# A four-block graph transformer on one core: edge counts built in SBUF, the output product woven into the next head, ten places for the turned count rows

## What is computed

```python
def _sparse_attention(x, src, dst, wq, bq, wk, bk, wv, bv, wo, bo):
    N, D = x.shape
    H, Dh = (NUM_HEADS, D // NUM_HEADS)
    q = (x @ wq + bq).reshape(N, H, Dh) * Dh ** (-0.5)
    k = (x @ wk + bk).reshape(N, H, Dh)
    v = (x @ wv + bv).reshape(N, H, Dh)
    scores = jnp.einsum('ehd,ehd->eh', q[src], k[dst])
    smax = jax.ops.segment_max(scores, src, num_segments=N)
    ex = jnp.exp(scores - smax[src])
    denom = jax.ops.segment_sum(ex, src, num_segments=N)
    attn = ex / denom[src]
    out = jax.ops.segment_sum(attn[:, :, None] * v[dst], src, num_segments=N)
    return out.reshape(N, D) @ wo + bo
...
for i in range(NUM_BLOCKS):
    y = _cond_layer_norm(x, cond, s1_w[i], s1_b[i], b1_w[i], b1_b[i])
    y = _sparse_attention(y, src, dst, wq[i], bq[i], wk[i], bk[i], wv[i], bv[i], wo[i], bo[i])
    x = x + y
    y = _cond_layer_norm(x, cond, s2_w[i], s2_b[i], b2_w[i], b2_b[i])
    y = jax.nn.relu(y @ m_w1[i] + m_b1[i]) @ m_w2[i] + m_b2[i]
    x = x + y
```

## Time and profile before

| what | us |
|---|---|
| median of 3 runs | 3600.6 |
| lowest and highest | 3591.68, 3606.22 |
| the profiled execution | 3616.84 |
| its span in the trace | 3615.1 |
| sorting, to the first one-hot tile | 144.8 |
| group loop | 247.2 |
| exchange, to the first product of block 0 | 112.2 |
| a block (the second of four) | 512.0 |
| graph layers | 1072 |

### The profile page before, as it was taken

The page is one execution under the profiler, slowest core; times in us unless marked ns, Lnnn a source line. Parts: engine busy times, 40 slices in busy tenths (PEclk is TensorE's granted clock), DMA queues, the critical chain, the costliest instruction groups (busy, mean ns, idle before and its releaser), DMA issues.

```text
span 3615.1 us, 31865 instructions
## 1 busy us (share of the span) xinstructions
PE 3073.9 (85%) x12190; PEld 1990.3 (55%) x12190; DVE 1745.2 (48%) x3292; ACT 749.7 (21%) x1046; POOL 832.6 (23%) x622
## 2 busy tenths in 40 slices
PE   4877349999899998999998899998286598898999
PEld 0344236777457766556676567765144355565555
DVE  9968324554235455234553245552288788412111
ACT  0132121222212222112222212222110211212221
POOL 5623121334223333213343213342010100000100
PEclk9988669999999999999999999999589599799899
DMA  4011210000000000100000100000435445201000
GB/s 139 5 32 30 76 54 12 1 24 1 30 26 12 1 24 18 36 14 1 24 1 18 38 12 1 24 1 29 104 111 151 128 131 148 61 14 56 12 0 29
DMA packets 83679, 147.31 MB, mean 41 GB/s; under 512 B 22047, under 2 KB 22438, under 8 KB 83528
## 3 DMA queue, kind: packets, MB, share of 16 engines
q1 hardware_dynamic: 61604, 121.16, 10.9%
q0 software_dynamic: 20624, 20.99, 2.1%
q10 hardware_dynamic: 1300, 3.13, 0.3%
HBM read 126.95 MB, written 30.37 MB: 44 GB/s over the span
## 4 chain that ended last, share of the span: by engine, by line
PE 67%; DVE 12%; issue 7%; DMA 4%; DVEq 4%; ACT 4%; POOL 1%; SPq 1%; POOLq 0%; ACTq 0%
PE ps L1269 14%; PE ps L1278 11%; PE ps L1362 9%; PE ps L1464 7%; PE ps L1419 4%; DVEq L912 3%; DMA typed_t<-run,rowi 3%; PE ps L1350 3%; DVE big L910 3%; PE ps L1351 3%; PE ps L1353 3%; PE ps L1352 3%; PE ps L1335 2%; PE ps L1456 2%; PE ps L1303 2%
## 5 line engine op out<-in xcount | busy, mean ns | idle before, releaser
L576 POOL TENSOR_TENSOR pacc<-pacc,prob 125x628 f32<-125x628 f32 (+1 forms) x288 | 405.4, 1408 | 301.2 <-DVE prob L862 301.2
L1278 PE MATMUL ps<-yT,w 128*128 128x416 f32 (+1 forms) x1152 | 407.0, 513 | 5.4 <-ACT yT L1077 5.4
L1362 PE MATMUL ps<-prob,big 125*128 125x314 f32 x1280 | 394.3, 429 | 11.1 <-DVE prob L862 11.1
L1464 PE MATMUL ps<-pieces,counts_r 125*125 125x512 f32 x1400 | 361.1, 414 | 27.3 <-DVE x L937 15.6
L834 DVE CUSTOM_DVE_ANT_0 ps<-ps,mneg 125x628 f32<-125x628 f32 x320 | 260.1, 823 | 243.9 <-PE ps L1335 243.9
L1115 ACT ACTIVATE prob<-ps 125x628 f32<-125x628 f32 x320 | 222.2, 694 | 710.9 <-PE ps L1353 710.9
L1464 PEld LDWEIGHTS ps<-pieces,counts_r 125*125 125x125 f32 x1400 | 264.0, 190 | 120.2 <-DVE x L937 22.3
L862 DVE SCALAR_TENSOR_TENSOR prob<-prob,ct 125x628 f32<-125x628 f32 x320 | 274.2, 857 | 95.6 <-ACT prob L1115 95.6
L1278 PEld LDWEIGHTS ps<-yT,w 128*128 128x128 f32 x1152 | 216.8, 189 | 187.0 <-issue 178.9
L1269 PE MATMUL ps<-w,yT 128*125 128x512 f32 x640 | 291.3, 602 | 11.5 <-DVE pieces L924 10.8
L1269 PE MATMUL ps<-w,big 128*125 128x512 f32 x640 | 282.9, 601 | 3.7 <-issue 3.0
(11 more groups left out here) (196 smaller groups left out, 4215.1 us busy)
## 6 DMA issues: line engine op xcount, KB each, us to landing
basis<-in_basis SPq DMA_DIRECT2D x240, 256.0 KB, 2.6
w<-in_m_w SPq DMA_DIRECT2D x8, 1024.0 KB, 6.7
typed_t<-zero_row SPq DMA_DIRECT2D x20, 305.2 KB
ct<-typed_t POOLq DMA_DIRECT2D x2, 3051.8 KB, 42.8
w<-in_wv SPq DMA_DIRECT2D x5, 1024.0 KB, 5.4
w<-in_wq SPq DMA_DIRECT2D x5, 1024.0 KB, 5.2
w<-in_wk SPq DMA_DIRECT2D x5, 1024.0 KB, 5.7
oT<-in_cw SPq DMA_DIRECT2D x9, 512.0 KB, 6.2
```

The costliest lines, as they stand in the source:

```text
L576: nc.gpsimd.tensor_tensor(pacc[:, c0:c0 + nn], pacc[:, c0:c0 + nn], prob[:, n % 3, p0:p0 + nn], ALU.add).then_inc(psum_done, 1)
L1278: last = mm(lin_ps(job, 128, nn), weight[:, k, m * 128:(m + 1) * 128], lhs[:, k, c0:c0 + nn], start=(k == 0), stop=(k == KD - 1))
L1362: last = mm(o_halves[:, b, :], vrow[:, t, h * DH:(h + 1) * DH], prob[:, n % 3, b * QUARTER:(b + 1) * QUARTER], start=(t == 0), stop=(t == ...
L1464: last = mm(lin_ps(job, P, D), counts_r[:, slot, k, :], pieces[:, piece, k, :], start=(self_ is None and k == 0 and piece == 0), stop=(k = ...
```

## The change

Three changes in one. **One:** the counts are built in SBUF. A tensor `typed` of 125 partitions and 2 x 6256 int32 words holds all 20 buckets; its halves are seen as `ct` and as `typed1` in float16, and the second half later as the mask `mneg`. POOL clears it once at the start (a MEMSET of 125x12512). POOL no longer scatters: for each group it loads the place of the group's bucket into a register and copies `run` there (625 int32 words, the place given by the register); a later group of the same bucket overwrites the partial sum. `run` has four places instead of two. The zero rows, the 20 zeroing DMAs, the 59 indirect DMAs and the ten loads are gone; type 1 is written to DRAM (`ct2_d`) by five DMAs, which must have landed before `mneg` overwrites it. In the group loop the four `onehot_dst` of a group are made by one TENSOR_TENSOR of 128x500, and `carry` is made by ACT behind its copy. After the mean layer POOL makes the counts of type 0 by ten subtractions `ct - ct2` in place of the load. **Two:** the ten output products of head h go into the first ten steps of head h + 1, one behind each step, and DVE's additions likewise; the last head's stay where they were. The six projections of head h + 2 are cut in parts of 1, 3 and 2. **Three:** the turned rows have ten places (two in `yT`, eight in `big`, both unused then), and SP, not ACT, starts their DMAs, in its queue behind the five of type 1.

```diff
+PARTS = {None: range(6), 0: range(0, 1), 1: range(1, 4), 2: range(4, 6)}
...
     for h in range(HEADS):
-        project(h + 2)
+        if h:
+            g["out"][h - 1] = [w.take() for _ in range(T)]
+        project(h + 2, 0)
+        project(h + 2, 1)
         max_row(h + 1)
         g["den"][h] = w.take()
-        g["out"][h] = [w.take() for _ in range(T)]
+        project(h + 2, 2)
+    g["out"][HEADS - 1] = [w.take() for _ in range(T)]
...
-            for s in range(2):
-                sp.wait_ge(rows_out[s], 16 * ((GROUPS + 1 - s) // 2))
+            sp.wait_ge(bucket_placed, GROUPS)
             for t in range(0, T, 2):
-                for r, to in ((0, ct), (1, typed1)):
-                    sp.dma_start(to[:, t:t + 2, :], typed_t[r * N + t * P:r * N + (t + 2) * P, :]
-                                 .rearrange("(t p) n -> p t n", p=P)).then_inc(typed_in[t // 2], 16)
+                sp.dma_start(ct2_d[t * P:(t + 2) * P, :].rearrange("(t p) n -> p t n", p=P),
+                             typed1[:, t:t + 2, :]).then_inc(ct2_out[t // 2], 16)
+            for s in range(T):
+                sp.wait_ge(crow_copied, s + 1)
+                sp.dma_start(crow_d[s * P:(s + 1) * P, :], turned_counts(s)).then_inc(crow_out[0 if s < 2 else 1], 16)
...
             drained_inc(consts_set)
+            nc.gpsimd.memset(typed[:], 0)
             pool.wait_ge(payload_ready, 1)
...
-                nc.gpsimd.indirect_dma_start(
-                    out=typed_t, out_offset=bass.IndirectOffsetOnAxis(ap=rowi[0:P, g:g + 1], axis=0),
-                    in_=run[:, g % 2, :], in_offset=None,
-                    bounds_check=2 * N - 1, oob_is_err=False).then_inc(rows_out[g % 2], 16)
+                place = pool.value_load(placei[0:1, g:g + 1], min_val=0, max_val=(PLACE + (T - 1) * N) // 2)
+                if g:
+                    pool.wait_ge(bucket_placed, g)
+                nc.gpsimd.tensor_copy(typed[:, bass.ds(place, N // 2)],
+                                      run[:, g % RUNS, :].bitcast(I32)).then_inc(bucket_placed, 1)
...
-            late_load(ct[:], count_rows(typed_t[0:N, :]), g["mean1"][-1], ctr_in)
+            pool.wait_ge(lin_full, g["mean1"][-1].full)
+            pool.wait_ge(ct2_in, 16)
+            for t in range(T):
+                nc.gpsimd.tensor_tensor(ct[:, t, :], ct[:, t, :], ct2[:, t, :], ALU.subtract)
+            nc.gpsimd.drain().then_inc(ct0_ready, 1)
             norm_power(11)
...
             for g in range(GROUPS):
+                if g >= 2:
+                    dve.wait_ge(onehot_used, STEPS * (g - 1))
+                V.tensor_tensor(onehot_dst[:, g % 2, :, :], col_iota[:, 0:P].unsqueeze(1).to_broadcast([128, STEPS, P]),
+                                es[:, 1, g * STEPS:(g + 1) * STEPS].unsqueeze(2).to_broadcast([128, STEPS, P]), ALU.is_equal)
                 for j in range(STEPS):
                     n = g * STEPS + j
                     if n >= 4:
                         dve.wait_ge(onehot_used, n - 3)
-                    V.tensor_scalar(onehot_dst[:, n % 4, :], col_iota[:, 0:P], es[:, 1, n:n + 1], None, ALU.is_equal)
...
             for s in range(T):
                 dve.wait_ge(crow_copied, s + 1)
-                V.tensor_scalar(mneg[:, s, :], crow[:, s % 2, :], 0.0, -BIG, ALU.is_equal, ALU.mult).then_inc(mneg_ready, 1)
+                if s % 2 == 0:
+                    dve.wait_ge(ct2_out[s // 2], 16)
+                V.tensor_scalar(mneg[:, s, :], turned_counts(s), 0.0, -BIG, ALU.is_equal, ALU.mult).then_inc(mneg_ready, 1)
...
-                if g >= 2:
-                    act.wait_ge(rows_out[g % 2], 16 * (g // 2))
-                A.activation(run[:, g % 2, :], ps[0:P, (g % 2) * 1536:(g % 2) * 1536 + N], ACT.Copy).then_inc(run_ready, 1)
+                if g >= RUNS:
+                    act.wait_ge(bucket_placed, g - RUNS + 1)
+                A.activation(run[:, g % RUNS, :], ps[0:P, (g % 2) * 1536:(g % 2) * 1536 + N], ACT.Copy).then_inc(run_ready, 1)
+                if g + 1 < GROUPS:
+                    A.activation(carry[:, (g + 1) % 2, :], ident16[:], ACT.Copy, scale=same[0:P, g:g + 1]).then_inc(carry_ready, 1)
...
                 for h in range(HEADS):
+                    row_written(h)
                     for j in range(2 * T):
                         exp_scores(h, j)
                         if h + 1 < HEADS:
+                            if j == 0:
+                                projected(h + 1)
                             max_scores(h + 1, j)
                         if j:
                             weighted_values(h, j - 1)
+                        if h and j < T:
+                            if j == 0:
+                                pe.wait_ge(o_copied, at(i, 2 * HEADS, 2 * h))
+                                if h == 1:
+                                    pe.wait_ge(w_in[0], at(i, 32, 32))
+                            attended(h - 1, j)
+                    if h + 2 < HEADS:
+                        project(h + 2, 0)
                     weighted_values(h, 2 * T - 1)
                     if h + 2 < HEADS:
-                        project(h + 2)
+                        project(h + 2, 1)
                     if h + 1 < HEADS:
                         max_row(h + 1)
```

187 lines of the change are left out of this document (99 added, 88 removed).

## The result

The changed kernel takes 3499.7 us (median, 3499.1 to 3500.6), the kernel before 3594.7 us over the same runs: a ratio of 0.9735 with a 95% interval of 0.9708 to 0.9762, 95 us less. A first series gave 3498.6, 3503.2 and 3508.1 us (ratio 0.9738) and, at a granted clock of 0.81 instead of 0.92, two slow executions of 3804.6 and 3806.4 us, which are left out. The forecast was 3494 us, with a range of 3438 to 3555. Medians of one kernel from different series lie up to 5 us apart (the kernel before 3592.5 to 3597.8, the changed one 3499.7 and 3503.2), so smaller differences of medians say little by themselves.

What follows compares the result with a forecast made beforehand. PE was read as holding 67% of the chain, with the group loop bound by the scatter's landing, then PE and DVE. Terms 9 - 35 - 48 - 48 + 15 = -107 us off 3600.6 gave 3494 us, range 3438 to 3555.

Steps and rivals of the forecast that it cites:

- The start: Before the group loop: POOL's larger MEMSET holds up DVE's first instruction, +9 us, between -1.4 and +9.8.
- The group loop: Group loop: scatter waits go, POOL's copy and DVE exclude each other at 3.0 us a group, -35 us.
- The exchange: Last group to block 0: load of `stage` waits behind turned rows in SP's queue, 64 against 112 us, -48 us.
- the ten places: Exchange: places for turned rows worth nothing beyond the rest, as the queue is later than ACT's copies.
- The blocks: Four blocks: woven output products and filled gaps gain 12 us a block, -48 us, between -24 and -80.
- The product's share: Blocks: weaving the output product itself gains 1.3 to 8.1 us a block, taken as 4; filled gaps 2.7 us.
- the row of maxima: Blocks: some half of the boundary idle time and the low clock behind the first go, some 5 us a block.
- The graph layers: After the blocks: POOL's subtractions stop DVE's mixing, 27 us, less 4 and 9, +15 us, between 0 and +27.
- (1): Group loop and graph layers: POOL and DVE share less kindly, 3.5 us a group and +27 us; 3535 us, chance 0.20.
- (4): Group loop: POOL becomes the bound, slower than before from 4.9 us a group; 3638 us at 5.5, chance 0.05.
- (2): Whole kernel: nothing collides, clock stays up, 2.67 us a group, no hold at the start; 3447 us, chance 0.20.
- (3): Blocks: weaving gains nothing, low clock moves and added products break the steps; 3602 us, chance 0.07.

Runs made afterwards that it cites:

- the second profile: The kernel before, unchanged, profiled once more for comparison by stage: one run, 3590.6 us.
- The double copy: Against the changed kernel, POOL copies each group's 625 words a second time, into a spare buffer: 3527.2 us, ratio 0.9805 to the kernel before.

## Why the prediction was right, step by step

The mechanisms came as forecast and the time, 3499.7 us, lies in the forecast's own range of 3465 to 3520. Against the second profile four of five terms came out dearer than their forecast, by 1 to 9 us, and one 6 us cheaper; one step is missing from the sum. That 3494 is only 6 us off is in part luck: the gain was 95 us, not 107, and the median from which it was taken, 3600.6 us, lies 6 us above that of the later runs.

*The start* (+9, measured +10.2): right in size and cause. Moving the MEMSET took it back.

*The group loop* (-35, measured -41.3). The waits for the scatter went, and DVE was next, as said. The pitch was sized at 3.0 us and is 2.86: POOL's copy takes 0.71 us alone and 0.8 to 1.0 us beside DVE, but only 0.47 us of it is lost to DVE. 58 x 0.14 = 8 us, where the difference is 6. The double copy shows that this term is real. The register load sets nothing, as the doubled work on POOL fits too.

*The exchange* (-48, measured -42.9). The load behind the queue was right: 12.5 us less without it, 9.9 of them in the exchange. Three things were mis-sized. The rows were given the 52 us of the loads; in the trace of the changed kernel their 2500 packets run from 359.3 to 417.1, 58 us, so the load of `stage`, issued at 45 us and 14.9 us long instead of 4.4, landed right behind them and 4 us late (60 us behind the last group, not 56); masks ended 33 us behind the last group, not 29; and the ten places were priced at nothing, though they are worth 8.5 us in the exchange and 11.6 in the median. The last didn't enter the sum wrongly, since the forecast's own chain ran masks beside the queue, but the reason given was not one.

*The blocks* (-48, measured -40.2 in one execution, -33.6 to -40.2 over those with the weaving). The product's share was sized at 4 + 2.7 - 1.2 = 5.5 us a block (1.2 of the 2.7 us of gaps belong to the cut projections) and is 19.3 / 4 = 4.8 alone. The term that was most oversized is the row of maxima: 5 + 1.2 us forecast, 15.5 / 4 = 3.9 measured. I took half of the idle time at the boundaries and the low clock behind the first as gone; the wait for the low parts stays (1.14 us before, 1.15 after), and so do the stretches at 0.84 to 0.86. That a low clock moves to whatever follows the gaps was said for the product, and it held: 6.8 us of lost clock a block were forecast to stay, and 7.0 are there, with the projections in it now.

*The graph layers* (+15, measured +23.5). The sum was 27 - 4 for the hold and 9 for the load that goes, rounded to 15. Measured, DVE's mixing was busy for 20.6 us more (205.7 - 185.1) and idle for 9.3 less, and the section took 11.1 us more: right in kind, 3 us too dear. What failed is the part that isn't there: the 9.15 us by which the first norm behind the blocks comes later. I had looked at the load of `ct` that went and not at the one of `ct2`, whose source changed, and the loads beside it.

*The baseline.* The differences were taken off the median, but the rows from a profile that was 22 us above the runs since. In the blocks this made head 0's product piece 12.1 us where the second profile has 10.7, so a part of the weaving's terms was drawn from stretches of lower clock that are not there as a rule.

*Rivals.* A pitch of 3.5 us (1) or over 4.9 us (4) didn't come; nor did 2.67 us with no hold at the start (2); the weaving gained (3). The graph layers came near to the +27 of rival 1, but 9 of their 23.5 us have another cause.

## What to carry to other kernels

When a wait is removed, price the next bound by who shares something with it: a POOL copy "beside" DVE cost DVE 0.47 us every group, a MEMSET 10 us once, ten subtractions 20 us; the last two were got back by moving the work to another place or other engines, not by making it shorter. In a chain of transfers, ask of each instruction ahead of the next load whether it needs to stand there: a queue and ten masks ahead of one load of weights were worth 24 us (70.1 to 46.1). Take a second profile of the kernel before when the one at hand lies above the median, ahead of reading small gaps from it: here the first one's blocks were 13.5 us longer at a lower granted clock.
